# Row maxima of the second attention from 64 rows a head, a head pair in two row tiles

## The reference

```
q = (layernorm(x) @ wq_w + wq_b)            # 4 x 512 x (16 heads * 64)
k = concat(ctx @ wk_w + wk_b, mk)           # 512 + 128 keys
v = concat(ctx @ wv_w + wv_b, mv)
attn = softmax(q @ k.T / sqrt(64))          # per batch and head, 512 x 640
x = x + (attn @ v) @ wo_w + wo_b
```

## Time and profile before

| | us |
|---|---|
| median of 3 runs | 1744.32 (1743.05 to 1745.8) |
| the profiled execution | 1748.7 |
| its span, first to last instruction | 1747.0 |
| TensorE busy | 1492.1 (85%) |
| VectorE busy | 904.9 (52%) |
| ScalarE, GpSimd busy | 494.4, 450.9 |
| second attention, opening to the last output | about 790 to 1575 |

### The profile page before, as it was taken

One profiled execution on the slowest core, in us unless ns is written; L12 is line 12 of the kernel. 1 busy time (PEld: TensorE's weight loads), 2 busy tenths in 40 slices (PEclk: granted clock), 3 DMA queues, 4 the chain that ended last, 5 costly groups with the idle time before them and its releaser, 6 DMA issues. The chain is left out here.

```text
span 1747.0 us, 18982 instructions
## 1 busy us (share of the span) xinstructions
PE 1492.1 (85%) x6088; PEld 884.1 (51%) x6088; DVE 904.9 (52%) x1684; ACT 494.4 (28%) x618; POOL 450.9 (26%) x257
## 2 busy tenths in 40 slices
PE   5889788898744988995599999999999999977886
PEld 2334334343344777782244446444554455535775
DVE  5556575665440000002557665766566655645666
ACT  2433333334211222220033332333233333320221
POOL 2000000000033000004044443445244533562333
PEclk7889899999956999997599999999999999986998
DMA  6521123202047454425466663565546653402001
GB/s 154 136 38 22 27 36 48 36 9 29 1 165 228 179 189 161 158 72 105 82 82 77 89 80 49 73 85 73 72 60 92 77 73 51 59 0 100 1 1 48
DMA packets 62237, 136.14 MB, mean 78 GB/s; under 512 B 10592, under 2 KB 21216, under 8 KB 57568
## 3 DMA queue, kind: packets, MB, share of 16 engines
q1 hardware_dynamic: 59440, 127.26, 39.1%
q0 software_dynamic: 2736, 8.13, 1.4%
HBM read 58.55 MB, written 12.06 MB: 40 GB/s over the span
## 5 line engine op out<-in xcount | busy, mean ns | idle before, releaser
L1063 POOL TENSOR_TENSOR a_probs<-a_probs 128x1024 f32<-128x1024 f32 x128 | 304.1, 2376 | 415.2 <-PE a_p_os L1626 414.7
L1134 ACT ACTIVATE a_probs<-a_p_s 128x1024 f32<-128x1024 f32 x160 | 163.8, 1023 | 378.5 <-PE a_p_s L1612 378.5
L417 DVE CUSTOM_DVE_ANT_0 a_scratch<-a_p_m,a_bias_q 128x512 bf16<-128x512 f32 x256 | 163.8, 687 | 117.8 <-PE a_p_m L572 117.8
L1345 DVE TENSOR_REDUCE a_max_ctx<-a_p_m 128x1 f32<-128x512 f32 x256 | 169.7, 687 | 79.6 <-PE a_p_m L1587 76.5
L327 ACT ACTIVATE a_probs<-a_p_s 128x1024 f32<-128x1024 f32 x128 | 130.6, 1024 | 175.2 <-PE a_p_s L597 174.7
L595 PE MATMUL a_p_s<-a_q_stack,a_k_stack 128*128 128x512 f32 x256 | 121.2, 500 | 28.5 <-DMA a_q_stack<-a_neg_max 28.5
L572 PE MATMUL a_p_m<-a_k_stack,a_q_stack 127*128 127x512 f32 x256 | 130.4, 555 | 13.6 <-DVE a_mx L417 7.0
L1626 PE MATMUL a_p_os<-a_probs,a_v 128*64 128x512 f32 x512 | 138.1, 618 | 0.0
L1507 PE MATMUL a_p_s<-a_o_raw,a_w 128*128 128x256 f32 x480 | 124.0, 393 | 13.8 <-DVE a_o_raw L1276 13.8
L1587 PE MATMUL a_p_m<-a_k_hl,a_q_hh 128*128 128x512 f32 x256 | 111.1, 481 | 18.3 <-DVE a_v L1323 8.1
L1281 DVE TENSOR_TENSOR a_yb<-a_p_os,a_yb 128x512 f32<-128x512 f32 x15 | 10.4, 691 | 219.1 <-PE a_p_os L1516 219.1
(11 more groups left out here) (200 smaller groups left out, 2135.9 us busy)
## 6 DMA issues: line engine op xcount, KB each, us to landing
a_w<-in_L_w SPq DMA_DIRECT2D x30, 1024.0 KB, 7.8
a_q_hh<-a_hi SPq DMA_DIRECT2D x64, 256.0 KB, 5.7
a_k_hl<-a_hi SPq DMA_DIRECT2D x32, 256.0 KB, 8.0
a_k_hl<-a_lo SPq DMA_DIRECT2D x32, 256.0 KB, 9.5
a_k_h<-a_hi SPq DMA_DIRECT2D x32, 256.0 KB, 10.6
a_q_lm<-a_lo SPq DMA_DIRECT2D x32, 256.0 KB, 7.1
a_ctx_t<-in_ctx_t SPq DMA_DIRECT2D x8, 512.0 KB, 5.6
a_q_stack<-a_hi SPq DMA_DIRECT2D x32, 128.0 KB, 4.8
```

Source lines behind the costliest of these rows:

```text
L417: dve.tensor_tensor_reduce(scratch[:, fill.n % M_BANKS, :], m, bias_q[:, i % NT, :], 1.0, -3.0e38, ALU.add, ALU.max, mx[:, i:i + 1]).then_ ...
L1063: pool.tensor_tensor(probs[:, kt], probs[:, kt - 1], probs[:, kt], ALU.add)\
L1134: act.activation(probs[:, kt, :, :], p_s[:, (KT1 * p + kt) % 2, :, :], ACT.Exp).then_inc(exp_done.sem, 1)
L1345: dve.tensor_reduce(max_ctx[:, NT * head + t:NT * head + t + 1], m, AX, ALU.max)\
```

## The change

Row maxima are now taken from the high parts alone: high part of q by high part of k, 64 rows instead of 128. So that a pair's two heads can lie in different halves of the rows, the second head's key stack has its halves exchanged (low part in rows 0 to 63, high part in rows 64 to 127); for the scores this makes no difference, since q's high part stands in both halves. Head 0's maxima use rows 0 to 63, head 1's rows 64 to 127. The step `i` now alternates between the heads, and `STEPS` puts the maxima in groups of two. Each key stack, the memory keys' too, takes five DMAs (four of 64 partitions for `k_hl`, one for `k_h1`) where there were three; the counts that wait for them follow (`KEY_PARTS`).

```diff
+        QUERY_PARTS, KEY_PARTS = 3, 5
...
-                 ("out", "score", "score", "value", "maximum", "maximum", "times_v", "maximum"),
-                 ("out", "maximum", "score", "score", "maximum", "value", "times_v", "maximum"),
-                 ("out", "maximum", "score", "score", "maximum", "times_v", "maximum", "rows"),
-                 ("out", "maximum", "total", "score", "turn", "score", "times_v"))
+                 ("out", "score", "score", "maximum", "maximum", "times_v", "value"),
+                 ("out", "score", "score", "maximum", "maximum", "times_v", "value"),
+                 ("out", "score", "score", "maximum", "maximum", "times_v", "maximum", "maximum", "rows"),
+                 ("out", "score", "maximum", "maximum", "total", "score", "turn", "times_v"))
...
+        def key_halves(stack, of):
+
+            return (of(stack[0:DK], 0), of(stack[DK:P], 1), of(stack[DK:P], 0), of(stack[0:DK], 1))
...
             def stack_key(p, n, landed):
-                for dst, part in ((k_hl[0:DK], hi), (k_hl[DK:P], lo), (k_h1[0:DK], hi)):
-                    sp.dma_start(dst[:, 2 * (p % HELD):2 * (p % HELD) + 2, :].bitcast(F32),
-                                 part[:, n, :].bitcast(F32)).then_inc(landed, 16)
+                s = 2 * (p % HELD)
+                for dst, part in zip(key_halves(k_hl, lambda half, i: half[:, s + i, :]),
+                                     (hi[0:P:2], hi[1:P:2], lo[0:P:2], lo[1:P:2])):
+                    sp.dma_start(dst.bitcast(F32), part[:, n, :].bitcast(F32)).then_inc(landed, 16)
+                sp.dma_start(k_h1[0:DK, s:s + 2, :].bitcast(F32), hi[:, n, :].bitcast(F32)).then_inc(landed, 16)
...
             def maximum(b, banks, p, i):
 
-                head, t = i // (NT + 1), i % (NT + 1)
+                head, t = i % 2, i // 2
                 s = 2 * (p % HELD) + head
+                rows = slice(DK * head, DK * (head + 1))
...
-                    done(pe.matmul(m, q_hh[:, s, P * t:P * (t + 1)], k_hl[:, s, :], start=True, stop=True))
+                    done(pe.matmul(m, q_hh[rows, s, P * t:P * (t + 1)], k_hl[rows, s, :], start=True, stop=True))
...
-                        mm = pe.matmul(m[:, MEM * t:MEM * (t + 1)], q_hh[:, s, P * t:P * (t + 1)],
-                                       mem_hl[:, head, p % PAIRS, :], start=True, stop=True)
+                        mm = pe.matmul(m[:, MEM * t:MEM * (t + 1)], q_hh[rows, s, P * t:P * (t + 1)],
+                                       mem_hl[rows, head, p % PAIRS, :], start=True, stop=True)
```

More of the change, by code:

```diff
@@ L874, in mixture_attention1 @@
         split_ready = Count(sem("split_ready"), 2 * PAIRS, first=1)
-        stacked = Count(sem("stacked"), 16 * 6 * PAIRS, -16 * 6 * BRING, first=1)
+        stacked = Count(sem("stacked"), 16 * (QUERY_PARTS + KEY_PARTS) * PAIRS, -16 * (QUERY_PARTS + KEY_PARTS) * BRING, first=1)
         mx_ready = Count(sem("mx_ready"), PAIRS, first=1)
@@ L942, in _ @@
             sp.wait_ge(filled_s, 1)
-            for dst, part in ((mem_hl[0:DK], hi), (mem_hl[DK:P], lo), (mem_h1[0:DK], hi)):
-                sp.dma_start(dst.rearrange("p i a n -> p i (a n)").bitcast(F32),
-                             part[:].rearrange("p a n -> p (a n)").bitcast(F32)).then_inc(mem_in, 16)
+            for dst, part in zip(key_halves(mem_hl, lambda half, i: half[:, i].rearrange("p a n -> p (a n)")),
+                                 (hi[0:P:2], hi[1:P:2], lo[0:P:2], lo[1:P:2])):
+                sp.dma_start(dst.bitcast(F32), part.rearrange("p a n -> p (a n)").bitcast(F32)).then_inc(mem_in, 16)
+            sp.dma_start(mem_h1[0:DK].rearrange("p i a n -> p i (a n)").bitcast(F32),
+                         hi[:].rearrange("p a n -> p (a n)").bitcast(F32)).then_inc(mem_in, 16)
             with sp.Fori(0, TURNS - 1) as i:
@@ L1118, in project @@
                 split_ready.wait(act, b, 2 * p + n - 1)
-                stacked.wait(act, b, 16 * 6 * p)
+                stacked.wait(act, b, 16 * (QUERY_PARTS + KEY_PARTS) * p)
                 if isinstance(b, int) and b == 0 and p == BRING:
                     for landed in q_first:
-                        act.wait_ge(landed, 16 * 3)
-                    act.wait_ge(k_first, 16 * 3 * BRING)
+                        act.wait_ge(landed, 16 * QUERY_PARTS)
+                    act.wait_ge(k_first, 16 * KEY_PARTS * BRING)
                 act.activation(hi[:, n, :], m, ACT.Identity, bias=bqk[:, n, p % PAIRS:p % PAIRS + 1])\
@@ L1172, in _ @@
             act.wait_ge(bqk_ready, 1)
-            act.wait_ge(mem_in, 16 * 3)
+            act.wait_ge(mem_in, 16 * KEY_PARTS)
             fill = Fill(PER - BASE)
@@ L1330, in split @@
                 if n == 0:
-                    stacked.wait(dve, b, 16 * 6 * p)
+                    stacked.wait(dve, b, 16 * (QUERY_PARTS + KEY_PARTS) * p)
                 if isinstance(b, int) and b == 0 and p == BRING:
                     for landed in q_first:
-                        dve.wait_ge(landed, 16 * 3)
-                    dve.wait_ge(k_first, 16 * 3 * BRING)
+                        dve.wait_ge(landed, 16 * QUERY_PARTS)
+                    dve.wait_ge(k_first, 16 * KEY_PARTS * BRING)
                 dve.scalar_tensor_tensor(out=lo[:, n, :], in0=m, scalar=bqk[:, n, p % PAIRS:p % PAIRS + 1],
@@ L1425, in open_split @@
                    .then_inc(split_ready.sem, 1)
-            dve.wait_ge(mem_in, 16 * 3)
+            dve.wait_ge(mem_in, 16 * KEY_PARTS)
             fill = Fill(PER - BASE)
@@ L1581, in maximum @@
                     if not isinstance(b, int) or b >= 0:
-                        stacked.wait(pe, b, 16 * 6 * (p + 1))
+                        stacked.wait(pe, b, 16 * (QUERY_PARTS + KEY_PARTS) * (p + 1))
                 if i == 0 and isinstance(b, int) and (b < 0 or b == 0 and p == RANK):
-                    pe.wait_ge(k_first, 16 * 3 * BRING)
-                    pe.wait_ge(q_first[p % PAIRS], 16 * 3)
+                    pe.wait_ge(k_first, 16 * KEY_PARTS * BRING)
+                    pe.wait_ge(q_first[p % PAIRS], 16 * QUERY_PARTS)
                 if t < NT:
-                    done(pe.matmul(m, q_hh[:, s, P * t:P * (t + 1)], k_hl[:, s, :], start=True, stop=True))
+                    done(pe.matmul(m, q_hh[rows, s, P * t:P * (t + 1)], k_hl[rows, s, :], start=True, stop=True))
                 else:
                     for t in range(NT):
-                        mm = pe.matmul(m[:, MEM * t:MEM * (t + 1)], q_hh[:, s, P * t:P * (t + 1)],
-                                       mem_hl[:, head, p % PAIRS, :], start=True, stop=True)
+                        mm = pe.matmul(m[:, MEM * t:MEM * (t + 1)], q_hh[rows, s, P * t:P * (t + 1)],
+                                       mem_hl[rows, head, p % PAIRS, :], start=True, stop=True)
                     done(mm)
@@ L1695, in _ @@
             pe.wait_ge(held.loaded, held.LOADS)
-            pe.wait_ge(mem_in, 16 * 3)
+            pe.wait_ge(mem_in, 16 * KEY_PARTS)
             pe.wait_ge(scaled, 1)
```

9 lines of the change are left out of this document (5 added, 4 removed).

## The result

| | before | changed |
|---|---|---|
| median, 20 runs of each | 1744.51 us | 1740.32 us |
| ratio, 95% interval | | 0.9978, 0.997 to 0.9987 |
| span of the profiled execution | 1747.0 us | 1735.1 us |
| last expert output to first exponential (the opening) | 83.6 us | 81.6 us |
| 30 of the 31 intervals between the pairs' reciprocals | 628.4 us | 622.9 us |

What follows compares the result with a forecast made beforehand. TensorE's queue was taken to bound the kernel; the terms -2.4 + 17.1 - 12.3 + 3 + 1.5 gave +6.9 us, from a median of 1744.3 to 1751.2 us. Its own range was 1745 to 1758 (chance 0.50), the wide one 1733 to 1768.

Steps and rivals of the forecast that it cites:

- first rival: Borders between full-array matmuls and row groups: row tiles cost no switch; 1732 us, range 1728 to 1740, chance 0.20.
- (b): New wait at kt 3: the second group of maxima waits 0.57 us for VectorE in 30 pairs; +17.1 us.
- (e): Key stack: five issues a key instead of three make two waits in the opening longer; +1.5 us.
- (a): Streams and tile switches on TensorE: pairing's gain nearly all spent on switches of 0.20 us; -2.4 us in all.
- (c): Even pairs: the second maximum behind `value` no longer waits for v's read, 0.82 us, 15 times; -12.3 us.
- (d): At kt 1 VectorE makes the `lo` splits late, so maxima wait in six places, 0.5 us each; +3 us.
- No switch: The first rival: row tiles cost no switch at borders with full-array matmuls; 1732 us, chance 0.20.
- one behind the other: Rival for the groups of maxima: row tiles don't overlap, each group streams 0.21 us longer; 1770 us, chance 0.12.
- loads in series: Rival for the groups of maxima: the row tiles' weight loads follow each other; +10 us, 1761 us, chance 0.10.
- nothing failed to pair: Refers to the rival that maxima don't pair at kt 1 and 2 or key stacks land late; 1765 us or more, 0.08.

Runs made afterwards that it cites:

- e11: The changed kernel without row tiles: new order and five transfers a key, maxima of 128 rows; 1741.38 us, ratio 0.9979 to the kernel before.
- e13: The changed kernel itself, run and profiled again; 1740.27 us, ratio 0.9974 to the kernel before.
- e12: The kernel before with kt 1 in the order of kt 2, `value` behind the maxima; 1733.27 us, ratio 0.9946 to the kernel before.
- e3: The kernel before with `turn` behind both scores in kt 4 instead of between them; 1738.48 us, ratio 0.9963 to the kernel before.
- e6: The kernel before with five transfers a key instead of three, nothing else; 1742.21 us, ratio 0.998 to the kernel before.
- e2: The changed kernel with the old list of steps, head after head: 64-row maxima, nothing paired; 1775.21 us, ratio 1.0161 to the kernel before.
- e4: The changed kernel with both heads' maxima in rows 0 to 63, one tile; 1765.61 us, ratio 1.0117 to the kernel before.
- e1: The kernel before with the new list of steps and alternating heads alone, 128 rows, three transfers; 1743.32 us, ratio 0.9995 to the kernel before.
- e5: The changed kernel with a `score` between the two groups of maxima at kt 3; 1749.45 us, ratio 1.0036 to the kernel before.
- e8: The changed kernel with the eight memory matmuls of kt 4 alternating between the heads; 1746.85 us, ratio 1.0013 to the kernel before.

## Why the prediction was wrong

The time was inside the wide range, 1733 to 1768, but below the forecast's own, 1745 to 1758, and the sign was wrong. It came out at the edge of the first rival's 1728 to 1740 by luck, for that rival's mechanism, a switch without a cost, is not what the traces show. The step that failed is the reading of the earlier trace rows: "The waits of the matmul queue there are small". The sum takes out only the wait for v and puts the second one of these rows, `turn` waiting for the join, at nothing, without a reason. It was worth 5.8 us in the 30 intervals. Beside it (b) was too large and (e) had the wrong sign.

By the steps of the forecast, in the 30 intervals, which hold 27 of the 30 pairs and 13 of the 15 waits for v (the forecast's terms are scaled to that; (e) is from the openings):

| step | forecast | found | from |
|---|---|---|---|
| (a) streams and tile switches | -2.2 | -3.0 to -3.6 | timelines; e11 and e13 |
| (b) new wait at kt 3 | +15.4 | +11.6 | 27 x 0.43 |
| (c) old wait for v | -10.7 | -10.7 | 13 x 0.82; e12: -9.7 |
| (d) VectorE late at kt 1 | +3 | +0.4 | 2 groups of 0.65 us |
| `turn` waits for the join | not in it | -5.8 | 21 turns; e3: -5.8 |
| bank for `out` behind kt 3's second group | not in it | +1.2 | 3 x 0.41 |
| sum of these | +5.5 | -6.6 | measured: -5.5 |
| (e) key stacks, opening | +1.5 | -2.0 to -2.7 | openings; e6, e11 |

The steady rows, with -3.3 for (a), come out 1.1 us lower than the 30 intervals, 0.04 us a pair; the terms aren't known better than that. With (e) the forecast for this part was +7.0 and the rows give -8.9. The 16 us between them are 5.8 from `turn`, 3.8 from (b), 3.8 from (e), 2.6 from (d) and 1.1 from (a) downwards, and 1.2 from the banks upwards. No one of them turns the sign alone; `turn` with any one of (b), (d) and (e) does. (The medians differ by 4.2 us, with an interval of 2.3 to 5.2. The whole stretch from the last expert output to the last reciprocal says 7.4 by the first profile after and 3.5 by e13, and the clock makes most of that difference.)

*(a) Right.* The mechanism was found as told: partners start together, 0.09 at each border and 0.11 of load behind it, 0.43 for a group against the 0.41 counted and 0.48 before. At the memory maxima the border cost less than counted: 0.95 until `total` for eight (1100.09 to 1101.04), and 0.09 ahead of them, against 8 x 0.11 = 0.88 counted in the earlier trace rows and a border of 0.20: that border was counted too high, and the group itself took 0.07 more. What the tiles save is 0.02 to 0.05 us in each of the three groups ahead of `times_v`, and nothing behind it, where VectorE sets the pace. e2 (+28 us against before) and e4 (+25 against the changed kernel) show how finely it is balanced: unpaired or in one tile, the same matmuls cost many times what pairing them brings. The Trainium skill (TensorEngine Tiling (Array Packing), Key Properties) says that a change of tiling mode drains the engine. The traces of e2 and of the changed kernel agree for row tiles with 0.09 us and an exposed load of 0.11; they don't show whether the 0.09 is a drain.

*(b) Right in its place, too large by a quarter.* 24 of the 30 second groups of kt 3 last 0.86 to 0.88 us from start to `score`, where the paired ones ahead of `times_v` last 0.43. So the wait is 0.43, not 0.57. What was mis-sized: "the two banks are emptied at s + 1.12 and s + 1.81" took VectorE's second read as a whole 0.69 behind the first. Two reads in a row take 1.29 us together in the timeline, not 1.38, so the second bank could be streamed into at s + 1.87 instead of s + 1.99; TensorE itself was there at s + 1.44, not 1.41 (s = 1097.13 + 0.11 for the load, 1097.24). What I told of its cause was right but narrow: e1 has no such wait and no gain from it, for the same 4.26 us pass in another place.

The six groups that are followed by `out` or `rows` instead of a score take 1.27 to 1.37: they wait another 0.41 or more for the bank. For the three of `out` that is new, and I had counted no cost for it. For the three of `rows` it isn't: before, TensorE waited there for the same bank, three times, 1.7 us together.

*(c) Right.* All 15 waits are gone from the list, of which the 30 intervals hold 13, 10.7 us at 0.82 each. e12, which removes this wait and gets some for `lo`, shows 9.7 there.

*(d) Nearly nothing.* The reserve of 3 us rested on the norm of the next batch standing ahead of the two `lo` splits. The groups ahead of `times_v` take 0.42 to 0.45 in 86 places and 0.65 in two; two more wait for `lo`, 2.6 us together, both outside the 30 intervals (the longer one where before had a wait of 1.6 us for `lo`):

```profile
PE a_p_m L1597 <- DVE a_lo L1345: 2.6, 2, 2.2
...
PE a_p_m L1607 <- DVE a_mx L1363: 0.7, 1, 0.7
```

*(e) Wrong in its sign.* "each longer by 0 (if bytes set it) to 1.2 us (two issues)" left a gain out, and no row excluded one. Five transfers of smaller pieces land earlier than three: 10.6 us for `k_h` before, 8.8 after and 8.4 in e6. All nine openings with five transfers last 80.2 to 81.8 us, all five with three 83.1 to 83.6. Why smaller pieces land earlier isn't shown here.

*The missing term.* It stood in the earlier trace rows: 3.5 us of waits for `mx`, 12 times. I put it among the small ones, for it is small by the list, and looked neither at the distance from `score` to `turn`, by which 24 turns are late, nor at how long the join takes. It was 0.69 to 0.76 us for eight columns. By the profile's rows 24 of the 32 joins before begin while GpSimd adds, and all 24 end 0.02 to 0.03 us after its end; the 8 others take 0.17. After, GpSimd's addition starts at 1098.73 and is over at 1101.09, the join at 1102.11 is never met by it, and takes 0.17 in all 32. That, and the place of `turn` behind both scores, takes its wait away: the list above shows one of 0.7 us. e3 moves `turn` alone and leaves the join as long as it was, and gets 5.8; so the new place is enough. A shorter join would have served as well, by the kernel before itself: the six turns of its loop whose join took 0.17 start 0.23 or 0.24 behind `score`. The Trainium skill (SBUF — State Buffer, SBUF: two separate sides) calls the port pair that VectorE and GpSimd share an exclusive lock, held for a whole instruction, for a VectorE operation with two SBUF inputs against a GpSimd one that reads SBUF. The trace agrees with it 24 times of 24 for the join (ends 0.02 to 0.03 us behind GpSimd's) and 31 of 31 for the product (ends 0.55 us behind); the maxima, with one input and that in PSUM, keep their 0.69.

*The rivals.* "No switch" falls by the 0.09 at the borders and by e2; "one behind the other" and "loads in series" by the record of two matmuls in 0.50 and two loads in 0.19, and by e4; nothing failed to pair. The ending that came true, faster by a wait not counted, was none of them. A rival "the order of `turn` saves the wait for the join" was there to be made from the earlier trace rows.

*What stays open.* The longer intervals of single executions all have a stretch at a granted clock of 0.50, mostly behind a wait of TensorE; why the same wait is followed by a fall in one execution and not in another is open, and so is how much of it stands in the medians. Also open are the 1.1 us by which the rows of the table miss the 30 intervals, and why smaller pieces land earlier.

## What to carry to other kernels

A wait that is small in the list of waits can hide an operation that takes four times its time: look at the longest against the shortest of a line, at what runs on the engine that shares its port, and at the distance between the starts around the wait. Before a longer interval is explained, look at the clock granted in it: in e4 and e8 it made 6 us. Tiles that pair two matmuls pay only where what they save exceeds the border at both ends; for two matmuls of 512 columns it is nearly even, while moving two steps out of a wait (e3, e12) cost nothing and brought 16 us. When reads are bunched on the engine that empties the banks, it sets the pace there, and a saving on the other engine (e5, e8) only moves the wait.

## What the runs showed of the hardware

- VectorE's join of 8 columns, from SBUF to SBUF: 0.17 us by itself, 0.68 to 0.77 when GpSimd's addition of 1024 columns (2.36 us) is under way; it ends 0.02 to 0.03 us behind it (24 of 24).
- VectorE's product of 512 columns, both inputs in SBUF: 0.69 us by itself, 0.75 to 1.71 when it begins during GpSimd's addition; it ends 0.55 us behind it (31 of 31, before).
- Two maxima of 512 columns from PSUM in a row take 1.29 us, one alone 0.69, with GpSimd or without.
- Two row tiles of 64 rows by 512 columns: 0.43 us from start to the next operation, both loads in 0.19; in one tile 0.65; a single one 0.42 (e2, e4).
- Eight 128-column matmuls in two row tiles: 0.95 us until the next operation when four follow four, 0.60 when they alternate (e8).
- A 256 KB copy within SBUF lands 10.6 us after its issue behind two of 256 KB, and 8.4 us behind four of 128 KB (medians of 32, before and e6).
- 6.8 us at a granted clock of 0.50 in the loop made the pairs that they touch some 3 us longer (e4, e8, e13); the falls came behind a wait of TensorE of 0.65 us (e13) or behind `rows` (e4, e8).
